# A fused attention and mixture-of-experts block: two DRAINs of GpSimd taken out, gelu's table, the offset and the fill of tile 0 placed a slot earlier, and batch 0's maxima placed ahead of batch 1's query

## What is computed

```python
mod = (silu(c) @ wmod).reshape(16, 6, 1, 128)      # shift, scale, gate; twice
h = layernorm(x) * (1 + ca) + sa
Q = h @ Wq + bq                                     # keys and values are Q too
x = x + ga * (softmax(Q @ Q.T / sqrt(128)) @ Q)     # for each batch
h = layernorm(x) * (1 + cb) + sb
route = sigmoid(h @ Wr + br)
e = argmax(route)                                   # one expert for each token
x = x + gb * max(route) * (gelu(h @ W1[e]) @ W2[e])
```

## Time and profile of the kernel before

| | |
|---|---|
| median of three runs | 363.1 us |
| the profiled execution's own time | 363.31 us |
| its span, from first to last instruction | 361.2 us |
| TensorE busy, matmuls | 327.5 us, 91% |
| VectorE busy | 270.6 us, 75% |
| ScalarE busy | 206.0 us, 57% |
| GpSimd busy | 189.6 us, 52% |
| mean granted TensorE clock | 0.97 |
| chain that ended last, on TensorE | 58% |
| the same, "issue" | 8% |

### The profile page before, as it was taken

How to read it: one execution, slowest core, us unless ns; L and a number is a source line. 1 busy time by engine, 2 the same in 40 slices (tenths; PEclk the granted TensorE clock), 3 DMA queues, 4 the chain that set the end, 5 groups by cost and what they waited for, 6 DMA issues and landing times.

```text
span 361.2 us, 7847 instructions
## 1 busy us (share of the span) xinstructions
PE 327.5 (91%) x2390; PEld 293.4 (81%) x2390; DVE 270.6 (75%) x1130; ACT 206.0 (57%) x438; POOL 189.6 (52%) x233
## 2 busy tenths in 40 slices
PE   4978999999999999999969887799999998899991
PEld 3657888888888888888858877799999898889991
DVE  5757898899988998889856685499877576568661
ACT  3477888878788788878644443253434334224340
POOL 5022055765567555765254357655655554654654
PEclk9999999999999999999996989699999999999997
DMA  3592223463565359415539016434887552543500
GB/s 111 154 232 87 59 56 119 128 124 119 109 98 145 143 159 284 137 54 161 88 118 352 25 69 196 140 102 133 277 287 229 170 151 66 154 117 91 163 22 17
DMA packets 34345, 49.16 MB, mean 136 GB/s; under 512 B 4304, under 2 KB 25971, under 8 KB 34304
## 3 DMA queue, kind: packets, MB, share of 16 engines
q1 hardware_dynamic: 27328, 31.66, 34.5%
q0 software_dynamic: 6368, 16.92, 12.6%
q10 hardware_dynamic: 608, 0.08, 0.1%
HBM read 28.15 MB, written 20.96 MB: 136 GB/s over the span
## 4 chain that ended last, share of the span: by engine, by line
PE 58%; DVE 17%; issue 8%; another core or an unknown queue 5%; POOL 4%; ACT 3%; DVEq 3%; DMA 1%; POOLq 0%; SPq 0%; ACTq 0%
PE mixed L664 10%; PE mixed L562 10%; PE side L584 3%; PE scores L548 3%; DVE row_max L1054 3%; PE side L505 2%; DVE gated L1223 2%; POOL sorted_rows L1586 2%; PE side L513 2%; DVEq L1185 2%; PE flipped L649 2%; PE flipped L548 2%; PE scores L647 2%; PE scores L648 2%
## 5 line engine op out<-in xcount | busy, mean ns | idle before, releaser
L1586 POOL DMA_INDIRECT sorted_rows<-payload,slots x64 | 70.3, 1099 | 74.1 <-DVE slots L1164 50.4
L1608 POOL DMA_INDIRECT out_dram<-y_out,tokens x71 | 75.1, 1058 | 55.8 <-DVE y_out L1230 34.8
L664 PE MATMUL mixed<-down_slot,hidden 128*128 128x128 f32 x568 | 74.3, 284 | 4.5 <-ACT hidden L884 3.6
L664 PEld LDWEIGHTS mixed<-down_slot,hidden 128*128 128x128 f32 x568 | 69.6, 198 | 6.0 <-ACT hidden L884 4.5
L562 PEld LDWEIGHTS mixed<-v_sb,probs_t 128*128 128x128 f32 x512 | 64.8, 194 | 8.2 <-issue 6.7
L562 PE MATMUL mixed<-v_sb,probs_t 128*128 128x129 f32 x512 | 70.2, 280 | 1.0 <-ACT probs_t L825 1.0
L817 ACT ACTIVATE shift<-ident,row_max 128x128 fp32r<-128x128 f32 x64 | 25.6, 401 | 27.4 <-DVE row_max L1054 21.4
L869 ACT ACTIVATE f_hi<-side 128x256 fp32r<-128x256 f32 (+1 forms) x39 | 14.3, 366 | 44.0 <-PE side L626 25.8
L1198 DVE CAST up_slot<-w_parts 128x1024 fp32r x39 | 27.2, 697 | 10.9 <-PE flipped L649 5.2
L884 ACT ACTIVATE hidden<-flipped 128x512 f32<-128x512 f32 x38 | 21.9, 599 | 14.0 <-PE flipped L649 6.8
L1054 DVE TENSOR_REDUCE row_max<-scores 128x1 f32<-128x512 f32 x32 | 21.9, 685 | 10.2 <-PE scores L538 10.2
(11 more groups left out here) (223 smaller groups left out, 808.1 us busy)
## 6 DMA issues: line engine op xcount, KB each, us to landing
rows<-sorted_rows SPq DMA_DIRECT2D x32, 388.0 KB
x_tile<-in_L_attn_inputs_dram SPq DMA_DIRECT2D x16, 256.0 KB
payload<-stored_gates SPq DMA_DIRECT2D x16, 256.0 KB, 8.5
sorted_rows<-pad_rows SPq DMA_DIRECT2D x9, 388.0 KB
w_parts<-in_L_ffn_W_dram SPq DMA_DIRECT2D x1, 2048.0 KB, 10.0
rows<-sorted_rows SPq DMA_DIRECT2D x7, 194.0 KB
out_dram<-y_out,tokens POOLq DMA_INDIRECT x71
sorted_rows<-payload,slots POOLq DMA_INDIRECT x64
```

The costliest lines, as they stand in the source:

```text
L664: last = nc.tensor.matmul(mixed[t % 2][:, u * H:(u + 1) * H], hidden[:, t % 2, f, u * P:(u + 1) * P], down_slot[:, t % 3, f, :], start=(f ...
L1586: nc.gpsimd.indirect_dma_start(rows_dram, bass.IndirectOffsetOnAxis(ap=slots[:, c:c + 1], axis=0), payload[:, b.q, j, :], None).then_inc(s ...
L1608: nc.gpsimd.indirect_dma_start(out_rows, bass.IndirectOffsetOnAxis(ap=tokens[:, t % RING, u:u + 1], axis=0), y_out[:, t % RING, u, :], Non ...
```

## The change

Four edits. The DRAIN ahead of the scatters of batches 11 and 13 goes. VectorE loads tile 0's offset in slot 14 ahead of batch 15's third maximum, and fills tile 0's weights in the same slot behind the second-norm moments of batch 14's first two blocks; both leave the tail. ScalarE does a gelu of one column behind batch 14's normalization and ahead of its router input. In the head and in slot 0, TensorE's score of batch 0's last block precedes batch 1's projection, and batch 1's first score precedes batch 0's first mix; VectorE's last two maxima of batch 0 precede the statistics of batch 2; ScalarE's last two shifts of batch 0 precede batch 1's query.

```diff
@@ tiles in SBUF @@
+        gelu_first = sb("gelu_first", [P, 1])
@@ TensorE: slot(k) @@
-                mix(now, 0)
-                score(after, 0)
                 if k == 0:
+                    score(after, 0)
+                    mix(now, 0)
                     flip_xn(after2)
                 else:
+                    mix(now, 0)
+                    score(after, 0)
                     project(after2)
@@ TensorE: the head @@
             score(first, 2)
+            score(first, 3)
             project(second)
-            score(first, 3)
             subtract_max(first)
@@ ScalarE: the head @@
             make_shift(first, 1)
-            query(second)
             make_shift(first, 2)
             make_shift(first, 3)
+            query(second)
@@ ScalarE: the tail @@
             normalize2(last_but_one)
+            nc.scalar.activation(gelu_first[:], shift1[:, 0:1], ACT.Gelu)
             router_input(last_but_one)
             gelu(0)
@@ VectorE: slot(k) @@
                     split_w1_lo(e)
+                if k == B - 2:
+                    dve.wait_ge(early_ready, 1)
+                    load_offset(0)
                 find_max(after, 2)
                 find_max(after, 3)
...
                 ln2_moments_of(now, 0)
                 ln2_moments_of(now, 1)
+                if k == B - 2:
+                    dve.wait_ge(w1_split, E)
+                    dve.wait_ge(w2_loaded, 16)
+                    fill_slots(0)
                 invert_den(now, 1)
@@ VectorE: the head @@
             find_max(first, 1)
+            find_max(first, 2)
+            find_max(first, 3)
             ln1(batch_at(2))
             variance1(batch_at(2))
-            find_max(first, 2)
-            find_max(first, 3)
@@ VectorE: the tail @@
             choose(before_these, 5)
-            dve.wait_ge(early_ready, 1)
-            dve.wait_ge(w1_split, E)
-            dve.wait_ge(w2_loaded, 16)
-            fill_slots(0)
             split_lo(0)
@@ GpSimd: scatter(b) @@
-                if b.n in (B - 5, B - 3):
-                    pool.drain()
                 wait(pool, slots_ready, b.n + 1)
```

## The result

| | before | after |
|---|---|---|
| median of 19 runs each | 362.6 us | 364.2 us |
| lowest and highest | 357.7, 367.6 | 361.7, 369.1 |
| profiled execution, span | 363.31, 361.2 | 367.31, 365.5 |
| from tile 0's down product to the end of the span | 152.1 us | 159.5 us |

The ratio is 1.0073, with a 95% interval from 1.0042 to 1.0104: 0.7% slower, where 2.1% faster was forecast. The profiled execution of after counts as a slow one, 3.1 us above its own median, so if all of that lies in its tiles, about 156 us is their more usual length (an estimate).

What follows compares the result with a forecast made beforehand. TensorE, by far the busiest engine, was taken as the bound. 4.7 - 0.9 - 0.1 + 1.0 + 1.3 + 1.3 + 0.6 = 7.9 us off 363.3 gave 355.4 us, range 353.4 to 360.2.

Steps and rivals of the forecast that it cites:

- The step that failed: Long run of tiles: the 7.9 us gained ahead of them should stay, since the tiles' waits are relative to each other.
- First DRAIN, the register load and the fill: Slot 14: removing the DRAIN gains 4.7 us; loading tile 0's offset there costs 0.9 and filling its weights 0.1.
- Tail and table: Ahead of tile 0: moving offset and fill out gains 1.0 us, loading the gelu table earlier 1.3 us.
- the rival of the slow clock: Slot 14: two idle spells of TensorE slow its clock, giving 357.7 us in all; chance 0.22.
- Clock at tile 0: Tile 0's sixteen matmuls: both idle spells ahead go, so TensorE keeps its clock; gain 1.3 us.
- Head: Head, batch 0: the last shifts precede batch 1's query, so the exponentials end sooner; gain 0.6 us.
- GpSimd waits anyway: Attention scatters: without the DRAIN the wait returns inside a scatter, losing the 4.7 us, for 360.1 us; chance 0.12.
- the wait that grows: Batch 12's scatter: GpSimd's wait grows 0.2 us per transfer to 10.0 us, for 364.8 us; chance 0.05.
- The slower end: Whole kernel: the change makes it slower than before; chance 0.05, against 0.91 for faster and 0.04 for same.

Runs made afterwards that it cites:

- before_third: The kernel before, unchanged, traced on a chip where no TensorE signal is held; its profiled span is 343.0 us.
- after_fourth: The kernel after, unchanged, on a chip where no TensorE signal is held; 339.5 us, ratio 0.9809 to the kernel before.
- after_third: The kernel after, unchanged, on a chip where no TensorE signal is held; 340.4 us, ratio 0.9853 to the kernel before.
- after_again: The kernel after, unchanged, measured again on a chip that holds TensorE's signals; 359.8 us against 360.8, ratio 0.9996 to the kernel before.
- before_again: The kernel before, unchanged, measured again on a chip that holds TensorE's signals; 360.8 us, profiled span 361.6 us.
- drain_only: The kernel before with only the two DRAINs of the attention taken out; 344.8 us, ratio 0.9956 to the kernel before.
- all_but_drain: The kernel after with the two DRAINs of the attention put back; 340.6 us, ratio 0.9857 to the kernel before.
- tail_only: The kernel before with only the one-column gelu and tile 0's offset and fill moved; 342.3 us, ratio 0.9921 to the kernel before.
- no_traffic: The kernel after with no output rows written and, from tile 6 on, only 32 of 256 rows loaded; 333.2 to 334.3 us.
- head_only: The kernel before with only the order in slot 0 and the head changed; 344.2 us, ratio 0.9955 to the kernel before.

## Why the prediction was wrong, point by point

**The step that failed** is the one that has no row: "All of it is ahead of the long run of tiles, whose waits are relative to each other, so it should stay." On the first chip 4.7 us had arrived by tile 1, none was left at tile 4, and after was 6.3 us behind at tile 23; the tiles took 159.5 us instead of 152.1 in the profiled executions. On quiet chips the sentence held (4.6 us at the first down product, 4.8 at the end). What the traces show is that TensorE's signals are held there in both kernels, for several us at a time, and that both steps of the loss are such holds. The first, at tiles 3 and 4, is in one of the two traces of after on holding chips. The second, at tile 23, is in both (7.9 and 3.8 us). It stands behind the DRAIN after tile 16, which the change itself made longer: after 98 transfers instead of 46 its gap grew from 4.62 to 8.89 us, outputs pile up, and GpSimd then issues ten transfers 0.3 us apart. The kernel before issues six or eight there before its first pause of 1.0 or 1.2 us. That gap is as long on quiet chips, where TensorE, busy for 40.00 of 40 us from 280 on (before_third and after_fourth), covers it. So the two removed DRAINs may have been paid for at the third. That is argued from two pairs of traces: no kernel with the DRAINs back, or without the one at tile 16, ran on a holding chip. Not settled either is why after is slower on the first chip (interval 0.4 to 1.0%) and not on the second (0.4% faster to 0.4% slower).

**On quiet chips the forecast was too high as well**, 7.9 us against 5.7 and 6.3. Between before_third and after_third, which has no slow spell of the clock ahead of its tiles, the first down product moves by 6.0 us (207.86 to 201.87): 0.9 up to slot 12's router, 3.1 in slot 14 and 2.1 from there. The clock's 1.3 is missing, 0.6 of the 3.7 and 0.2 of the 2.3; the head gave 0.3 more.

**First DRAIN, the register load and the fill: 3.7 forecast.** 15.98 - 12.3 = 3.7 on the first chip, 3.0 on a quiet one, where the kernel before loses less clock (14.54 us). The mechanism was right. In after_again slot 14 takes 14.07 us from router to router (15.17 in before_again), with a slow spell of the clock from 184.09 on. Alone the removal takes slot 14 to 10.8 us (router at 182.34, next at 193.12 in drain_only), so load and fill cost 0.7, forecast 1.0. But with the DRAIN in, the wait for the root hides them (the slot takes 12.6 to 13.4 us in three of the four traces of all_but_drain, and 14.8 in the first, which has a slow spell of the clock in it, as the traces of before have). So much of what taking the DRAIN out could bring was already there, and on top of the other edits it brought only 0.5 and 1.5 us.

**Slots 12 and 13** were not in the sum; they cost 1.7 us on the first chip (0.7 and 1.0, against 11.3 us each), and their routers' signals came 0.9 and 1.1 us late. In after_again, too, 12.0 us pass from slot 12's router to slot 13's, where every trace but these two has 11.4.

**Tail and table: 2.3 forecast.** On a quiet chip the way from slot 14's router to the first down product goes from 11.49 (before_third) to 9.15 us (tail_only: 196.26 to 205.41), so 2.3, as forecast. In after_third it is 9.42, in after_fourth only 10.73, with a slow spell of the clock from 193.89 on. On the first chip 0.8 (9.74 to 8.95 from slot 15's first mix), with TensorE slow: mixes of 1.93 and 1.38 us at 198.67 and 200.57 instead of 1.05. This is the rival of the slow clock, by its effect, and 10.73 - 9.42 = 1.3 us is the price that it named: three of four traces of after have such a spell of 3.4 us between 184 and 201. The table load takes 1.28 us at 200.08 and the activation behind it starts at 201.37, 0.01 us after its end. The flush of about 1.38 us that the Trainium skill (ScalarE: Activation LUTs, What ACT_TABLE_LOAD costs) counts besides shows in no row here.

**Clock at tile 0: 1.3 forecast.** 1.1 on the first chip (3.14 to 2.02), nothing on a quiet one, where before runs it in 2.05. Its size came from one execution. drain_only has the slow spell there (3.68 us), after the same two idle spells that left before_third at full clock: with the DRAIN's idleness out, the slow spell that before_third has at 189.6 stands at 205.4 instead, over tile 0. It takes 1.6 us there and explains much of why that edit alone brought 1.5 us (by the ratio) and not the 3.8 of its slot. One trace shows it.

**Head: 0.6 forecast, within bounds of 0.3 and 1.2.** 0.3 between the first two traces (router of slot 12 at 170.13 and 169.87). Over the sixteen traces (no_traffic apart) that router starts at 170.1 to 171.0 without the edit and at 169.1 to 170.2 with it, so some 1.0 us is the fairer figure, and head_only brought 0.45%, 1.6 us. In the traces of after the first subtraction came at 19.3 to 19.7 us and not at 18.9, since the last shifts now wait for their maxima. ScalarE, kernel after:

```profile
18.44 0.40 ACT L820 ACTIVATE shift<-ident,row_max 128x128 fp32r<-128x128 f32 x1 [0.35 <-DVE row_max L1058]
19.13 0.40 ACT L820 ACTIVATE shift<-ident,row_max 128x128 fp32r<-128x128 f32 x1 [0.29 <-DVE row_max L1058]
```

**GpSimd waits anyway, and the wait that grows.** No such wait in the attention, with 98 transfers and no DRAIN. The DRAIN itself does cost more behind more transfers: a gap of 4.62 us behind 46 and of 8.89 behind 98, the same on both kinds of chip; yet 8.5 us behind the first 44. The prediction took the DRAIN's wait for one for transfers under way. no_traffic speaks against it:

```profile
L1621 POOLq DRAIN  x3: 594/596/5843, 266.9 to 316.9; - x3
```

The first of these takes 5.84 us at 266.9, though GpSimd's last indirect transfer is issued by 221.8, its last packet has ended by 223.1, and 64 had been issued in all. The other two, with none since, take 0.6 us. So the wait is not for transfers under way. The count alone does not give it either: 5.8 to 6.2 us behind 46, 5.84 behind 64, 10.1 to 10.7 behind 98, 6.9 to 8.7 behind the first 44. The slower end came out, and a longer wait of GpSimd may have a part in it, but at the DRAIN that stayed, after tile 16, and not in a scatter, where the prediction had looked for it.

## What to carry to other kernels

A gain at the front is worth what the last stage lets through: before writing "it stays", list the longest waits of that stage, and take "remote" and "issue" among them as a warning that something is in charge there that the sum doesn't hold. The spread of 2.7% among the runs of before was a hint of it here. A cost that is taken out at one place may wait at the next: the DRAIN that stayed took 10.1 us instead of 6.2. A wait that is removed may have been the cover of other work, and its idleness may go with where the clock falls; so cost the edits together and not one by one. And where a result contradicts a sum that the trace confirms stage by stage, measure both kernels on another chip before looking for a fault in the edit.

## What was not expected of the hardware

The same program takes 346 us in some measurements and 361 to 363 us in others, on other chips of the same type (whether it is the chip or its state is not shown), with the attention alike (slot 12 begins within 1 us) and the tiles taking 135.1 us (before_third) or 151.9 us (before_again). What differs in the traces is TensorE's signals, which on the slower chips reach the other engines up to 9.4 us after the recorded end of the work, and several at once. Mean granted clocks of 0.97 and 0.99 look like its consequence more than its cause: the slow spells follow idle ones. The tiles' loads were not slower there: a 1552-byte packet of a tile's rows took 66 ns at the median on both.
